# A two-layer graph kernel on one core: the short row block's products go to four column groups of the PE array, and its layer 1 part moves to the start of layer 1

## The reference, cut to what matters

```python
def layernorm(x): m, v = mean(x), var(x); return (x - m) / sqrt(v + 1e-5)

def layer0(input, A, h0, y):                    # input 5000x128, A 5000x5000 of 0/1, y one-hot 5000x16
    adj = A * (y @ y.T)                         # edges inside a class
    adj = adj / maximum(sum(abs(adj), axis=1), 1e-12)
    return 0.9 * (adj @ input) + 0.1 * h0

def layer1(h, adj, W_proj, b_proj, W_gcn, b_gcn):
    sim  = tanh(adj * adj) * (adj > 0)          # tanh(1) where there is an edge
    # the 350 largest of a row are kept; a row of this data has fewer edges than that
    h2   = tanh(h @ W_proj + b_proj)
    return relu(sim @ (h2 @ W_gcn) + b_gcn)

x = layernorm(x + layer0(x, adj, h0, y))
x = layernorm(x + layer1(x, adj, ...))          # output 5000x128 float32
```

## Time and profile before

| | |
|---|---|
| time, median of 3 runs (lowest to highest) | 467.72 us (467.58 to 469.69) |
| the profiled execution's own time | 467.99 us |
| its span, first instruction to last | 466.2 us |
| busy: PE, DVE, ACT, POOL | 437.5, 377.8, 263.8, 160.0 us |
| granted PE clock, mean | 0.987 of 2.4 GHz |
| moved by DMA | 108.50 MB, nearly all of it in the first 55% of the span |

### The profile page before, as it was taken

One profiled execution on the slowest core, in us unless ns is written; L12 is line 12 of the kernel. 1 busy time (PEld: TensorE's weight loads), 2 busy tenths in 40 slices (PEclk: granted clock), 3 DMA queues, 4 the chain that ended last, 5 costly groups with the idle time before them and its releaser, 6 DMA issues.

```text
span 466.2 us, 15130 instructions
## 1 busy us (share of the span) xinstructions
PE 437.5 (94%) x5104; PEld 387.8 (83%) x5104; DVE 377.8 (81%) x1358; ACT 263.8 (57%) x355; POOL 160.0 (34%) x310
## 2 busy tenths in 40 slices
PE   3669999999999999999999999999999999999994
PEld 2448988888888988888888887888888888888883
DVE  5988999999999999999999976675576576576562
ACT  4997998989999999999999934900000000000000
POOL 3012543555444455544445541221211221221222
PEclk9987999999999999999999999999999999999999
DMA  8999999999999999999999200000000000000000
GB/s 263 409 414 423 420 419 415 405 389 413 417 419 426 422 422 412 421 424 416 423 417 426 63 2 1 13 11 17 17 11 17 17 11 17 17 11 17 17 12 23
DMA packets 25518, 108.50 MB, mean 233 GB/s; under 512 B 5097, under 2 KB 15490, under 8 KB 15490
## 3 DMA queue, kind: packets, MB, share of 16 engines
q1 hardware_dynamic: 25490, 108.14, 57.4%
HBM read 105.57 MB, written 2.56 MB: 232 GB/s over the span
## 4 chain that ended last, share of the span: by engine, by line
PE 75%; DVE 11%; issue 6%; ACT 5%; DMA 2%; POOL 1%; DVEq 0%; POOLq 0%; SPq 0%; ACTq 0%
PE acc L522 64%; PE words L472 6%; DVE a_bits L783 3%; DMA a_rows<-in_adj_dram 2%; DVE turned L870 2%; PE feat_acc L585 2%; PE proj_acc L596 2%; ACT count_out L679 2%; ACT count_out L686 2%; PE xnt_acc L577 1%; DVE g_words L320 1%; ACT count_out L755 1%; DVE z_high L921 1%; ACT count_out L747 1%; DVE same_class L893 1%
## 5 line engine op out<-in xcount | busy, mean ns | idle before, releaser
L522 PE MATMUL acc<-x_parts,turned 128*128 128x257 f16 (+1 forms) x1600 | 192.9, 277 | 4.8 <-DVE turned L870 3.8
L679 ACT ACTIVATE count_out<-a_rows,ones 128x2688 bf16<-128x2688 f32 (+1 forms) x80 | 190.1, 2377 | 0.5
L522 PEld LDWEIGHTS acc<-x_parts,turned 128*128 128x128 fp8e4 (+1 forms) x1600 | 155.1, 99 | 28.1 <-issue 5.2
L522 PE MATMUL acc<-f_parts,turned 128*128 128x256 f16 (+1 forms) x1560 | 171.6, 273 | 0.8 <-DVE turned L870 0.8
L522 PEld LDWEIGHTS acc<-f_parts,turned 128*128 128x128 fp8e4 (+1 forms) x1560 | 152.0, 98 | 19.2 <-issue 1.3
L783 DVE TENSOR_SCALAR a_bits<-a_rows 128x2688 bf16<-128x2688 f32 (+1 forms) x80 | 116.8, 1460 | 2.4 <-DMA a_rows<-in_adj_dram 2.0
L422 POOL TENSOR_TENSOR var_eps<-mean_var,consts 128x1 f32<-128x1 f32 x80 | 18.5, 232 | 268.0 <-DVE mean_var L1077 139.8
L870 DVE TENSOR_SCALAR turned<-a_words 128x320 uint16 (+1 forms) x305 | 66.5, 232 | 53.6 <-PE acc L522 53.2
L425 POOL TENSOR_TENSOR rstd<-var_eps,consts 128x1 f32<-128x1 f32 x80 | 86.4, 1080 | 6.3
L870 DVE TENSOR_SCALAR turned<-same_class 128x320 uint16<-128x320 uint16 x313 | 71.1, 253 | 0.1
L472 PEld LDWEIGHTS words<-pack,a_bits 128*128 128x128 bf16 (+1 forms) x1600 | 51.6, 97 | 9.3 <-DVE a_bits L783 7.4
(11 more groups left out here) (110 smaller groups left out, 288.1 us busy)
## 6 DMA issues: line engine op xcount, KB each, us to landing
a_rows<-in_adj_dram SPq DMA_DIRECT2D x39, 1344.0 KB, 7.9
a_rows<-in_adj_dram SPq DMA_DIRECT2D x39, 1156.0 KB, 8.3
out_dram<-xn SPq DMA_DIRECT2D x39, 64.0 KB, 1.5
h_rows<-in_L_gnn_h_dram SPq DMA_DIRECT2D x19, 128.0 KB, 8.0
xs<-in_x_dram SPq DMA_DIRECT2D x3, 640.0 KB, 10.2
xs<-in_x_dram SPq DMA_DIRECT2D x1, 512.0 KB, 9.0
y_nat<-in_L_gnn_y_dram SPq DMA_DIRECT2D x1, 304.0 KB, 3.6
a_rows<-in_adj_dram SPq DMA_DIRECT2D x1, 84.0 KB
```

Source lines behind the costliest of these rows:

```text
L522: mm = pe.matmul(acc[par][0:m, 0:cols], bits, parts[:, b, 0:cols], start=first and b == blocks[0], stop=last and b == blocks[-1])
L679: act.activation(count_out[0:m, 0:w], a_rows[par][h][0:m, 0:w], ACT.Relu, bias=ones[0:m, 0:1], scale=-HUGE, accum_out=col).then_inc(s_coun ...
```

## The change

The short block (`n` = 39 and `n` = 79) gets a path of its own.

- `multiply_short`: source block `b` goes to output partitions `b % 4 * 32` to `+ 8` of the bank, so that its weights are placed in column group `b % 4` of the array. Each group adds up ten of the 40 products.
- `gather_short`: ACT copies the four partial sums from their partitions to partitions 0 to 7 of a free input buffer (`a_rows[0][1]`), four instructions, and DVE adds them in one `tensor_reduce`.
- In layer 0, ACT does this at the start of its step 42, ahead of that step's `h_t`, and `row_scale`, `add_high` and `add_low` of `n` = 39 read the sum. PE's `early` for layer 1's block 1 waits for the four copies rather than for `s_z`.
- In layer 1 the short block's words are unpacked by one DVE instruction (`short_bits`) at the end of DVE's step 44. PE multiplies into the bank `gram_acc`, free by then, right after layer 1's block 1. ACT copies the parts after its five long instructions. DVE adds them at the end of its step 3 (`short_sum_of`), and makes `z` and the moments at the end of step 4 (`short_moments_of`). POOL makes `rstd` and the result after its step 6 (`short_block`), and SP stores it last, as before.
- Block 38 (`END`) is now the last with the usual path. POOL normalizes it, as it did the short block.

```diff
+    END = FULL - 1
+    QUADS = 4
...
@@ pool, step1
+            def short_block():
+                pool.wait_ge(s_short_dve, 6)
+                pool.tensor_tensor(short_var, short_moments[:, 1:2], ln_eps[0:TAIL, :], ALU.add)\
...
+                if isinstance(t, int) and t == 6:
+                    short_block()
+                if isinstance(t, int) and t - 2 == END:
...
@@ pe
             def multiply_ready(n, par):
                 pe.wait_ge(s_unpacked, n + 1)
-                if not isinstance(n, int) or n >= 2:
+                if isinstance(n, int) and n == NB + 1:
+                    pe.wait_ge(s_gathered, QUADS)
+                elif not isinstance(n, int) or n >= 2:
                     pe.wait_ge(s_z, n - 1)
                 pe.sem_inc(s_ready, 1)
+
+            def multiply_short(bank, bits, parts, cols, blocks):
+
+                for b in blocks:
+                    q = b % QUADS * 32
+                    mm = pe.matmul(bank[q:q + TAIL, 0:cols], bits[:, b, :].bitcast(F8)[:, 0:TAIL], parts[:, b, 0:cols],
+                                   start=b < QUADS, stop=b >= NB - QUADS)
+                return mm
...
+                    if t == 1:
+                        pe.wait_ge(s_short_bits, 1)
+                        multiply_short(gram_acc, short_bits, f_parts, 2 * F, range(NB)).then_inc(s_short_acc, 1)
                     return
...
@@ act
+            def gather_short(bank, cols, pitch):
+
+                for q in range(QUADS):
+                    act.activation(short[:, q * pitch:q * pitch + cols], bank[q * 32:q * 32 + TAIL, 0:cols], ACT.Copy)\
+                        .then_inc(s_gathered, 1)
...
+                if isinstance(t, int) and t == NB + 2:
+                    act.wait_ge(s_acc, NB)
...
+                    gather_short(acc[odd], PARTS, 260)
...
+            act.wait_ge(s_short_acc, 1)
+            act.wait_ge(s_short_dve, 1)
+            gather_short(gram_acc, 2 * F, 2 * F)
@@ dve
             def row_scale(n, par, m):
-                dve.wait_ge(s_acc, n + 1)
+                if isinstance(n, int) and n == LAST:
+                    dve.wait_ge(s_gathered, QUADS)
+                    dve.tensor_reduce(short_acc, short_parts[:, :, 0:PARTS].rearrange("p q c -> p c q"), AX.X, ALU.add)\
+                        .then_inc(s_short_dve, 1)
+                    dve.wait_ge(s_short_dve, 1)
+                else:
+                    dve.wait_ge(s_acc, n + 1)
...
+            def short_sum_of():
+
+                dve.wait_ge(s_gathered, 2 * QUADS)
+                dve.tensor_reduce(short_sum, short_halves[:, :, :].rearrange("p q c -> p c q"),
+                                  AX.X, ALU.add).then_inc(s_short_dve, 1)
...
                 if isinstance(t, int) and t == 3:
                     check_counts()
+                    short_sum_of()
                 if isinstance(t, int) and t == 4:
+                    short_moments_of()
                     check_sums()
```

More of the change, by code:

```diff
@@ L172, in packed_path @@
         turned_more = a_rows[0][0][:, 0:NB * LANES // 2].bitcast(U16).rearrange("p (b i) -> p b i", b=NB)
+        short = a_rows[0][1][0:TAIL, :]
+        short_parts = short[:, 0:QUADS * 260].rearrange("p (q c) -> p q c", q=QUADS)
+        short_halves = short[:, 0:2 * QUADS * F].rearrange("p (q c) -> p q c", c=F)
+        short_acc = short[:, 1040:1040 + PARTS]
+        short_sum, short_feat, short_z, short_xn = (short[:, 1300 + i * F:1300 + (i + 1) * F] for i in range(4))
+        short_stats = short[:, 1812:1818]
+        short_moments = short[:, 1818:1820]
+        short_var, short_rstd = (short[:, 1820 + i:1821 + i] for i in range(2))
+        short_bits = sb("short_bits", [P, NB, WORDS], U16)
         a_bits = [sb(f"a_bits{h}", [P, HB * P], BF16) for h in range(2)]
@@ L287, in packed_path @@
         s_sum = sem("s_sum")
+        s_short_bits = sem("s_short_bits")
+        s_short_acc = sem("s_short_acc")
+        s_gathered = sem("s_gathered")
+        s_short_dve = sem("s_short_dve")
+        s_short_pool = sem("s_short_pool")
         def turned_at(n, par):
@@ L376, in store @@
                 m = rows_of(t)
-                sp.wait_ge(s_result, t + 1)
-                sp.dma_start(rows_in(out, t, par, pair, slice(0, F)), xn[par][0:m, :]).then_inc(s_out[par], 16)
+                short_block = isinstance(t, int) and t == LAST
+                if short_block:
+                    sp.wait_ge(s_short_pool, 3)
+                else:
+                    sp.wait_ge(s_result, t + 1)
+                sp.dma_start(rows_in(out, t, par, pair, slice(0, F)), short_xn if short_block else xn[par][0:m, :])\
+                    .then_inc(s_out[par], 16)
             steps(sp, store, 0)
@@ L535, in multiply @@
                         multiply_blocks(n, par, m, parts, range(X_PART[q].start, X_PART[q].stop), q == 0, q == 3)
+                elif isinstance(n, int) and n == LAST:
+                    mm = multiply_short(acc[par], turned[:, par, :, :], parts, PARTS, blocks)
+                    if h == 1:
+                        mm.then_inc(s_acc, 1)
                 else:
@@ L634, in step1 @@
                         .then_inc(s_sum, 1)
+                    return
                 for h in range(2):
@@ L698, in words_of @@
                                    ACT.Copy).then_inc(s_words, 1)
+                if isinstance(t, int) and t == NB + 2:
+                    act.wait_ge(s_acc, NB)
+                    act.wait_ge(s_bits, 2 * END + 2)
+                    act.wait_ge(s_counted, 2 * END + 2)
+                    gather_short(acc[odd], PARTS, 260)
                 if valid(t - 1) and not (isinstance(t, int) and t <= 1):
@@ L906, in normalize_block, with sums @@
                 normalize(n, par, rows_of(n)).then_inc(s_xn, 1)
+            def sums(n, par, m):
+                return short_acc if isinstance(n, int) and n == LAST else acc[par][0:m, :]
             def row_scale(n, par, m):
-                dve.wait_ge(s_acc, n + 1)
+                if isinstance(n, int) and n == LAST:
[3 more added lines that the diff above has]
+                    dve.wait_ge(s_short_dve, 1)
+                else:
+                    dve.wait_ge(s_acc, n + 1)
                 dve.wait_ge(s_z, n)
-                dve.tensor_scalar(rs[0:m, 0:1], acc[par][0:m, 2 * F:PARTS], 2 * SCALE * L1_EPS,
+                dve.tensor_scalar(rs[0:m, 0:1], sums(n, par, m)[:, 2 * F:PARTS], 2 * SCALE * L1_EPS,
                                   1 / (1 - ALPHA), ALU.max, ALU.mult).then_inc(s_floor, 1)
@@ L920, in add_high @@
                 dve.wait_ge(s_xh, n + 1)
-                dve.scalar_tensor_tensor(z_high[0:m, :], acc[par][0:m, 0:F], rs[0:m, 1:2],
+                dve.scalar_tensor_tensor(z_high[0:m, :], sums(n, par, m)[:, 0:F], rs[0:m, 1:2],
                                          xh[par][0:m, :], ALU.mult, ALU.add).then_inc(s_zhigh, 1)
@@ L1027, in step @@
                 begin(NB + 4, 2, 0, BITS)
+                if isinstance(t, int) and t == NB + 4:
+                    dve.wait_ge(s_words, NB)
+                    dve.tensor_scalar(short_bits[:, :, :], words_at(LAST), ONE_BIT, ONE_PAIR,
+                                      ALU.logical_shift_left, ALU.bitwise_and).then_inc(s_short_bits, 1)
             steps(dve, step, LAG, {1: feature_ones, 3: bias, LAG: check_y_sums}, FIRST)
@@ L1042, in bits @@
                 def bits(lo, hi):
-                    if valid(t) and (not isinstance(t, int) or t > 2):
-                        unpack(t + NB, par, rows_of(t), words_at(t), lo, hi)
+                    if valid(t) and (not isinstance(t, int) or 2 < t <= END):
+                        unpack(t + NB, par, P, words_at(t), lo, hi)
                 bits(0, 2)
-                post = valid(t - 2)
+                post = valid(t - 2) and not (isinstance(t, int) and t - 2 == LAST)
                 if post:
-                    m = rows_of(t - 2)
+                    m = P
                     dve.wait_ge(s_acc, t + (NB - 1))
@@ L1078, in step1 @@
                 bits(10, 14)
-                if valid(t - 3) and not (isinstance(t, int) and t - 3 == LAST):
+                if valid(t - 3) and not (isinstance(t, int) and t - 3 >= END):
                     if not isinstance(t, int) or t >= 5:
                         dve.wait_ge(s_out[odd], (pair - 2 + par) * 16)
-                    normalize(t + (NB - 3), odd, rows_of(t - 3)).then_inc(s_result, 1)
+                    normalize(t + (NB - 3), odd, P).then_inc(s_result, 1)
                 bits(14, BITS)
```

32 lines of the change are left out of this document (24 added, 8 removed).

## The result

The changed kernel is slower: 472.21 us median against 467.75, a ratio of 1.0076 with a 95% interval of 1.0061 to 1.0091. The median counts one slow execution of 630.65 us, which showed a granted clock of 0.662 and which nothing here explains; the ratio leaves it out, and without it the median is 472.05. The ratio isn't the quotient of the two medians, which is 1.0095, so a loss in us is uncertain by about one: 3.6 by the ratio, 4.5 by the medians. The other runs spread from 470.03 to 473.18 us, those of the kernel before from 467.58 to 469.69. The measured time lies outside my range, 464.8 to 470.6. The profiled execution took 473.18 us, the most of these, with a span of 471.4, 5.2 more than before.

The account below looks back on a forecast made before the run. PE was taken to bound the kernel, busy 94% of the span, with ACT and DVE ahead of it before 307 us. +3.5 for block 5's later start and -4.1 for the tail gave -0.6: 467.1 us, range 464.8 to 470.6.

Parts of the forecast that it names:

- part 3: Layer 1's moved short block: DVE waits for ACT's copies ahead of block 4's unpacking, PE starts block 5 3.5 us later.
- part 2: Layer 0's short products in four column groups take 1.4 us; all that follows, until ACT's long instructions, is 2.4 us earlier.
- part 3, four copies behind the long instructions: In layer 1, ACT's four copies after its five long instructions take 4 x 0.31 us and a little, ending at 301.3.
- part 3, the reduction: DVE's layer 1 sum of the short block's parts: 512 elements at 1.03 ns each, 0.7 us.
- part 3, unpacking of block 4: DVE's unpacking with five other instructions, behind the reduction, takes 2.63 us; PE starts block 4 at 304.75.
- part 3, moments and checks: On DVE after block 4's unpacking: short_moments_of takes 1.33 us, then check_sums 1.54 us, ending at 307.5.
- DVE reads block 38: Start of the last DVE chain, at the end of layer 1, forecast at about 459.3 us.
- part 1: Removed tail products at the end: -4.51 us, +0.06 for DVE's larger instructions, +0.36 for the last store, together -4.1 us.
- rival 2: PE's 4.1 us idle gap ahead of block 4 lets its clock fall: +1.0 us, 468.1, or 469.6 at worst; chance 0.20.
- Rival 3: Column groups don't run side by side, so layer 0's 40 products take 4.4 us: +2.6 us, 470.3; chance 0.12.
- Rival 1: DVE's wait at the end of step 3 doesn't bind, PE starts block 5 at 305.0: 461.5 us; chance 0.08.

Follow-up runs that it names:

- the version with ACT's copies out of the way: Changed kernel with ACT copying layer 0's short-block parts after h_t and xn_t of its step 42, not ahead of them; 472.50 us, ratio 1.0095 to the kernel before.
- the version with a plain layer 0: Changed kernel with only its layer 1 half kept, layer 0's short block as in the kernel before; 473.90 us, ratio 1.0126 to the kernel before.
- the runs with PE kept busy: Changed kernel plus 44 unused 8-column products on PE right ahead of its wait for block 4's weights; 470.63 us, ratio 1.0049 to the kernel before.
- the late sum: Changed kernel with DVE's layer 1 short-block sum, the moments and POOL's part two steps later; 463.89 us, ratio 0.9918 to the kernel before.
- early store: Late-sum version with the short block's 4 KB stored after block 10, so block 38's 64 KB go last; with four groups 464.07 us, ratio 0.9920.

## Why the prediction was wrong

It said -0.6 us of span for the profiled execution, and +5.2 was measured. The mechanism and its place were right: in part 3, "DVE's reduction waits for these at the end of step 3, ahead of the unpacking of block 4", the gap in PE ahead of block 4, the main cost. The sum was not. Its terms:

| step | forecast | measured |
|---|---|---|
| part 2, ACT's last copy to `f_parts` | 2.4 us earlier | 0.04 earlier (0.47 from the short block's start) |
| part 3, four copies behind the long instructions | 1.35 | 1.45 |
| part 3, the reduction | 0.7 | 1.8 |
| part 3, unpacking of block 4 | 2.63 | 2.6 |
| part 3, moments and checks | 2.8 | 2.5 |
| DVE reads block 38 | 3.5 later | 7.23 later |
| part 1, the tail | -4.1 | -2.0 |

The span missed the forecast by 5.8 us: 2.0 by part 2, 1.1 by the reduction, 2.1 by the tail, 0.4 because this execution came to the short block later, and 0.2 by the rest of part 3 with the clock behind the gap.

- **The step that failed first is part 2**, "h_t ... 2.4 us earlier now. From there PE's sequence ... sets the pace". The products cost what I took for them (1.40 us on the chain for 1.4), and the sum was complete 1.95 us from the short block's start, as forecast (2.03). But each copy took 0.38 us and not 0.31, so `h_t` came 0.3 us later than I had it. While ACT copied, PE was idle for 1.75 us, its clock fell, and 18 products took 3.59 us instead of 2.13; by the execution in which it didn't fall, this took 1.1 us of the gain. I had rival 2, the clock, for the large gap only, and never priced this one. The last 0.5 us went to DVE, whose reduction stands ahead of `f_parts` in its queue: PE waits 0.63 us for it where the clock didn't fall, and 2.53 us in the version with ACT's copies out of the way.
- **The reduction in part 3** is an error of mine and of the row together. The sum of layer 1 has eight parts of 128 columns (high and low of four groups), 1,024 elements and not 512. And an element costs 1.8 ns here and not 1.03: the rows that I took the earlier trace rows add 16 and 40 neighbours each, this one eight numbers that lie 512 bytes apart. With the same stride 512 elements took 1.02 us; two parts 1,040 bytes apart, 514 elements, took 0.68. Which of stride and length of a sum makes the price, no run separates.
- **Rival 2, the clock behind the large gap**, came true: 0.50 from 308.5 to 311 us. I had +1.0 for it. It cost 0.3 us in the profiled execution and 1.8 in that of the version with a plain layer 0; by the runs with PE kept busy it is 1.3 us, give or take one. The gap was 5.36 us and not 4.1, because of the longer reduction; part 2 moved both its ends alike.
- **Part 1, the tail.** DVE, POOL and the first store are as forecast. "The 64 KB land ... inside the time that the last store takes anyway" failed, and so did the 0.33 us for the last issue. The path from POOL's result to the end grew by 2.4 us instead of 0.36: about 1.2 for the 64 KB, and the rest for an issue behind them, which took 2.06 us in this execution and 0.46 in another.
- **Rival 3 is refuted**: the groups run side by side, at 0.027 us a product.
- **Rival 1**, the wait doesn't bind, was rightly given little as a forecast. As an experiment it is what the late sum makes, and it gave 463.9 where I had worked out 461.5. Its profile lays the difference to the turn's lost gain, about 2.0 us, since PE was the bound from block 2 on, and to the longer tail, 0.7; it also came to the short block 0.2 us earlier.

The runs add up the loss from ratios, in steps of one edit or two. The short block moved, in one group, with a late sum and an early store: +0.10% (1.0010). Four groups in place of one: -0.90% (0.9920). The store back at the end: nothing that can be told (0.9918). The sum back ahead of block 4's unpacking: +1.58% (1.0076). So the groups brought about what the chain of the kernel before promised, 4 us, and the order on DVE cost nearly twice as much. The larger store at the end is inside the first of these steps, where it offsets what the short block's move off the end gave.

## What to carry to other kernels

When work is moved off the end, look where its last step lands in each engine's queue. Here one reduction of 1.9 us ahead of the unpacking cost 7.4 us, because it waited for an engine that had 13 us of its own work first, and everything behind it waited too. Putting it two steps later turned a loss of 0.8% into a gain of 0.8%. Splitting small products over column groups makes them cheap at once, but the partial sums have to be gathered: count their copies and the elements of the reduction, and try two groups before four. And treat an idle stretch of PE that a change opens as one that may be paid twice, in the wait and in the clock after it. Last, before two profiles are compared by their times, look for a moment ahead of the change and count from it: here it moved by up to 1.4 us between executions, more than several of the effects.

## What the runs showed of the hardware

- Column groups share the array fully: 0.109, 0.055 and 0.027 us a product of 8x256 with 128 rows in one, two and four groups. The last is below the 0.032 us of the 9-column products in the earlier trace rows, which I had taken for the floor of issuing. The Trainium skill (TensorE: Matmul & The Clock Gate, Packing small matmuls) lets weight loads overlap running products only where the row groups differ, and gives 2.38x for three column tiles. This case measured 4.0x for four in the steady pace and 3.6x for the 40 products as a whole (4.53 against 1.26 us), on the same row groups, so here the measurement decides against the rule on loads; three tiles no run here has.
- The clock's lower level came after 1.75 us of idle PE at 278 us (0.60 over the next 4 us) and after 2.65 us with two groups, but not after 0.93 us (the earlier trace rows had it at the end only after some 3.7 us). The length of the idle stretch alone doesn't settle it: of six profiles with the same 1.75 us at the turn, five had the lower level behind it, and one, shown above, didn't.

The two windows of the version with two groups, turn and gap:

```profile
280.00:284.00 4.00, 3.81 (x35) 3.34 (x34) 3.39 (x20) 1.32 (x5) 1.72 (x4) 1.00 0.01 4
...
304.80:308.00 3.20, 3.17 (x19) 2.44 (x20) 2.61 (x14) 0.00 (x0) 0.20 (x1) 0.65 0.07 20
```

- A store of 4 KB issued directly behind one of 64 KB held SP's queue for 0.46 to 2.43 us over eight profiles of the changed kernel and the experiments, against 0.33 us otherwise.
